# Causal attention, 16 heads: the order of a chunk's key tiles, passed tiles between kept ones

## The reference

```python
a = jax.nn.softmax(jnp.einsum('bhsd,bhtd->bhst', q, k) * D ** (-0.5), axis=-1)
if causal:
    s, t = (a.shape[-2], a.shape[-1])
    mask = (jnp.arange(t)[None, :] > jnp.arange(s)[:, None]).astype(a.dtype)
    a = a * mask
o = jnp.einsum('bhst,bhtd->bhsd', a, v)
```

## Time and profile before

| | us |
|---|---|
| median of 3 runs | 3826.64 |
| lowest and highest | 3819.09 and 3826.94 |
| the profiled execution, its own time | 3808.98 |
| its span, first to last instruction | 3807.2 |
| the stage of the change in it, from the first score to the last copy | 1283.7 to 2207.5 |

### The profile page before, as it was taken

One profiled execution on the slowest core, in us unless ns is written; L12 is line 12 of the kernel. 1 busy time (PEld: TensorE's weight loads), 2 busy tenths in 40 slices (PEclk: granted clock), 3 DMA queues, 4 the chain that ended last, 5 costly groups with the idle time before them and its releaser, 6 DMA issues. The chain is left out here.

```text
span 3807.2 us, 65854 instructions
## 1 busy us (share of the span) xinstructions
PE 3254.3 (85%) x23031; PEld 1440.8 (38%) x23031; DVE 2444.5 (64%) x4118; ACT 1976.2 (52%) x3961; POOL 1482.6 (39%) x795
## 2 busy tenths in 40 slices
PE   4999999526885899999999986599999998969998
PEld 2323332315773232232322254122222222647776
DVE  5878896563114778778788455466666672655665
ACT  2777777331112256666666744156666665523443
POOL 2000000353222231434325240377878777415553
PEclk7989998757996799999999888699999999969999
DMA  1000000286772100100000030100000000347445
GB/s 58 12 14 11 14 8 4 90 302 244 229 240 75 31 16 7 26 5 18 18 5 9 1 109 23 31 18 10 23 10 23 9 10 24 109 145 246 84 82 118
DMA packets 163212, 239.03 MB, mean 63 GB/s; under 512 B 35859, under 2 KB 132826, under 8 KB 155994
## 3 DMA queue, kind: packets, MB, share of 16 engines
q1 hardware_dynamic: 142698, 209.40, 17.4%
q0 software_dynamic: 19056, 24.88, 3.7%
q10 hardware_dynamic: 1152, 0.79, 0.1%
HBM read 136.44 MB, written 68.92 MB: 54 GB/s over the span
## 5 line engine op out<-in xcount | busy, mean ns | idle before, releaser
L1262 DVE TENSOR_REDUCE a_part_max<-a_wb 128x1 f32<-128x512 f32 x1024 | 641.5, 683 | 110.3 <-PE a_wb L1348 101.1
L1814 DVE TENSOR_REDUCE a_part_max<-a_mx 128x2 f32<-128x1024 f32 (+1 forms) x416 | 473.3, 1180 | 264.7 <-PE a_mx L1915 264.7
L1748 ACT ACTIVATE a_e<-a_sc 128x512 f32<-128x512 f32 (+1 forms) x832 | 451.3, 594 | 231.6 <-PE a_sc L1895 225.1
L748 DVE TENSOR_REDUCE xa_part_max<-xa_mx 128x2 f32<-128x802 f32 x512 | 469.7, 985 | 103.4 <-PE xa_mx L845 102.5
L1719 POOL TENSOR_TENSOR a_part_sum<-a_part_sum,a_e 128x2048 f32<-128x2048 f32 x112 | 509.0, 4545 | 53.5 <-ACT a_e L1748 43.4
L1206 ACT ACTIVATE a_e<-a_sc 128x512 f32<-128x512 f32 x640 | 349.4, 601 | 337.7 <-PE a_sc L1373 333.0
L692 ACT ACTIVATE xa_e<-xa_sc 128x512 f32<-128x512 f32 (+1 forms) x832 | 445.8, 596 | 114.1 <-PE xa_sc L832 106.3
L1348 PE MATMUL a_wb<-a_ks,a_qs 96*128 96x512 f16 x1024 | 405.3, 402 | 25.4 <-DVEq L1289 9.5
L1895 PE MATMUL a_sc<-a_qs,a_ks 97*128 97x512 f16 (+1 forms) x832 | 277.3, 397 | 15.5 <-DMA a_qs<-a_neg_max 7.0
L868 PE MATMUL xa_po<-xa_e,xa_v 128*32 128x256 f32 (+1 forms) x3328 | 274.0, 402 | 7.4 <-ACT xa_oc L735 2.6
L1151 POOL TENSOR_TENSOR a_em<-a_e,a_later 128x512 f32<-128x512 f32 x64 | 81.0, 1266 | 459.2 <-ACT a_e L1206 371.9
(11 more groups left out here) (397 smaller groups left out, 5187.9 us busy)
## 6 DMA issues: line engine op xcount, KB each, us to landing
experts_w_up<-in_we SPq DMA_DIRECT2D x32, 1024.0 KB, 6.5
wall<-expert_halves SPq DMA_DIRECT2D x18, 1088.0 KB, 9.8
experts_w_down<-in_we SPq DMA_DIRECT2D x32, 512.0 KB, 6.1
a_qs<-a_stage SPq DMA_DIRECT2D x360, 32.0 KB, 1.8
moe_xr<-sorted_rows SPq DMA_DIRECT2D x79, 136.5 KB, 2.1
a_ks<-a_stage SPq DMA_DIRECT2D x336, 32.0 KB, 1.9
choose_whole<-in_wm SPq DMA_DIRECT2D x18, 544.0 KB, 9.0
expert_halves<-choose_cut SPq DMA_DIRECT2D x18, 544.0 KB, 7.9
```

Source lines behind the costliest of these rows:

```text
L748: dve.tensor_reduce(part_max[:, 2 * h:2 * h + 2, t, c], src[:, :, :mxw], AX.X, ALU.max).then_inc(m_taken, 1)
L1262: dve.tensor_reduce(part_max[:, j, t, k:k + 1], src[:, :mxw], AX.X, ALU.max).then_inc(unit_taken, 1)
L1748: act.activation(e[:r, m % ering, j, :], src[:r, :], ACT.Exp, scale=scale).then_inc(s_taken, 1)
L1814: dve.tensor_reduce(dst, src, AX.X, ALU.max).then_inc(m_taken, 1)
```

## The change

The tiles of a chunk are put in another order, the same for all engines: the passed ones are spread evenly between the kept ones. `tiles` is the list in the new order, `place_of` the place of a tile in it; all waits and ring buffers count by that place. What each tile computes, the rings and the work for the chunks ahead stay. The orders (P passed, K kept): type 0 unchanged; type 1 K P K K K P K K K P K K K P K K; type 2 P K eight times; type 3 P P P K four times.

```diff
+    tiles = []
+    for n in range(NC):
+        skipped = sum(passed(n, kt) for kt in range(nkt))
+        kept = nkt - skipped
+        tiles += sorted(((n, kt) for kt in range(nkt)),
+                        key=lambda x: (2 * x[1] + 1) * kept if x[1] < skipped else (2 * (x[1] - skipped) + 2) * skipped)
+    place_of = {tile: m for m, tile in enumerate(tiles)}
...
-    tile_work = [PASSED_WORK if passed(m // nkt, m % nkt) else TILE_WORK for m in range(nkt * NC + 1)]
+    tile_work = [PASSED_WORK if passed(*tile) else TILE_WORK for tile in tiles] + [TILE_WORK]
...
-                for kt in range(nkt):
-                    if kt == TPC and n - 1 in carry_at:
+                for step, (_, kt) in enumerate(tiles[nkt * n:nkt * n + nkt]):
+                    if step == TPC and n - 1 in carry_at:
                         place_sums(n - 1)
...
-                            pool.wait_ge(pv_done, summed[nkt * before_n + before_kt + 1])
-                        pool.tensor_tensor(em[:, kt % 2, :, :], e[:, (nkt * n + kt) % ering, :, P * i:P * i + P],
+                            pool.wait_ge(pv_done, summed[place_of[before_n, before_kt] + 1])
+                        pool.tensor_tensor(em[:, kt % 2, :, :], e[:, place_of[n, kt] % ering, :, P * i:P * i + P],
...
-            for m in range(nkt * NC):
-                r = kt_rows[m % nkt]
+            for m, (_, kt) in enumerate(tiles):
+                r = kt_rows[kt]
...
-                dve.wait_ge(exp_done, HG * (nkt * n + TPC * (n % NCH)))
+                dve.wait_ge(exp_done, HG * (place_of[n, TPC * (n % NCH) - 1] + 1))
...
             def sum_values(n, kt):
-                m = nkt * n + kt
+                m = place_of[n, kt]
...
-                        sum_values((m - 1) // nkt, (m - 1) % nkt)
+                        sum_values(*tiles[m - 1])
                     elif m:
-                        sum_weights((m - 1) // nkt, (m - 1) % nkt)
+                        sum_weights(*tiles[m - 1])
```

More of the change, by code:

```diff
@@ L971, in passed @@
         return causal and kt < TPC * (n % NCH)
+    tiles = []
[5 more added lines that the diff above has]
+    place_of = {tile: m for m, tile in enumerate(tiles)}
     summed = [0]
-    for m in range(nkt * NC):
-        summed.append(summed[-1] + (not passed(m // nkt, m % nkt)))
+    for tile in tiles:
+        summed.append(summed[-1] + (not passed(*tile)))
     def adds_up(n, kt):
@@ L1145, in _ @@
                     if i is not None:
-                        pool.wait_ge(exp_done, HG * (nkt * n + kt + 1))
+                        pool.wait_ge(exp_done, HG * (place_of[n, kt] + 1))
                         if TPC * n + i >= 2:
                             before_n, before_kt = (n, kt - 2) if i >= 2 else (n - 1, TPC * ((n - 1) % NCH) + i + 2)
-                            pool.wait_ge(pv_done, summed[nkt * before_n + before_kt + 1])
-                        pool.tensor_tensor(em[:, kt % 2, :, :], e[:, (nkt * n + kt) % ering, :, P * i:P * i + P],
+                            pool.wait_ge(pv_done, summed[place_of[before_n, before_kt] + 1])
+                        pool.tensor_tensor(em[:, kt % 2, :, :], e[:, place_of[n, kt] % ering, :, P * i:P * i + P],
                                            later[:, :].unsqueeze(1).to_broadcast([P, HG, P]), ALU.mult).then_inc(masked, 1)
@@ L1154, in _ @@
                         m = nshared[n] + shared[n].index(kt)
-                        pool.wait_ge(exp_done, HG * (nkt * n + kt + 1))
-                        tile = e[:, (nkt * n + kt) % ering, :, :]
+                        pool.wait_ge(exp_done, HG * (place_of[n, kt] + 1))
+                        tile = e[:, place_of[n, kt] % ering, :, :]
                         if m:
@@ L1192, in _ @@
                         act.wait_ge(exp_done, HG * (m - ering + 1))
-                        n, kt = (m - ering) // nkt, (m - ering) % nkt
+                        n, kt = tiles[m - ering]
                         if kt in shared[n]:
                             act.wait_ge(pool_added, nshared[n] + shared[n].index(kt) + 1)
-                    n, kt = m // nkt, m % nkt
+                    n, kt = tiles[m]
                     if passed(n, kt):
@@ L1361, in score @@
             def score(n, kt, j):
-                i = HG * (nkt * n + kt) + j
+                i = HG * place_of[n, kt] + j
                 r = kt_rows[kt]
@@ L1430, in _ @@
             for m in range(nkt * NC + 1):
-                n, kt = m // nkt, m % nkt
-                if kt == 0 and n < NC:
+                n, kt = tiles[m] if m < nkt * NC else (NC, 0)
+                if m % nkt == 0 and n < NC:
                     pe.wait_ge(negmax_loaded, 16 * HG * (n + 1))
```

## The result

| | before | after |
|---|---|---|
| median of 16 runs each, side by side | 3826.79 | 3834.93 |
| lowest and highest | 3813.08 and 3845.80 | 3826.28 and 3858.75 |
| the profiled execution, its own time | 3808.98 | 3832.05 |
| its span | 3807.2 | 3830.2 |
| the stage of the change in it | 924.4 | 940.7 |

The ratio is 1.0035, with an interval of 1.0018 to 1.0052: the change makes the kernel slower by 0.35%, about 13 us (the two medians lie 8.1 apart). The forecast was 3820, no change within 0.2%; the range of 3797 to 3845 holds the time, the direction was wrong. In the profiled executions the stage is 16.3 longer; the other 6.7 of the span's 23.0 lie outside the stage, where by the clock's records PE stood at the lower level for 649 us after and 638 before. The profiled execution of before is faster than any of its 16 runs, so the spans differ by more than the medians.

What follows compares the result with a forecast made beforehand. PE was read as busiest (85%), but in the stage ACT paced passed tiles and PE kept ones. Terms -6.4 (type 1), -7.2 (type 2), +1.5 (type 3), +2 (chunk 15), -6 (clock), +9 (hand-overs) sum to -7.1: 3820, range 3797 to 3845.

Steps and rivals of the forecast that it cites:

- The bound and the two regimes: In the changed stage no engine is full: ACT's exponentials pace passed tiles (PE idle 0.7 each), PE bounds kept tiles.
- First, the gain in type 2: Passed tiles behind kept ones fill PE's 0.7 idle with products and sums: 5.9 us gained per type 2 chunk.
- fourth rival: Products follow a tile later, maxima stay heavier in kept tiles, so the weave doesn't mix; inside the forecast, no own chance.
- Second, the mask's exposure: PE stands 1.0 at diagonal value products, three more times a chunk in types 2 and 3; bounds 0 and 1.5.
- Type 1: Chunks of type 1: gain 3.1 less 1.5 for masks, net -1.6 a chunk, -6.4 for four.
- Type 3: Chunks 3, 7, 11: pairs of kept and passed tiles get longer, net +0.5 a chunk, +1.5 in all.
- Type 0 unchanged (62): Type 0 chunks, whose order is not changed, were to stay at 62 us.
- Chunk 15 (+2): Last chunk: 2 us less at the higher clock, 6 longer at the lower level; +2 was taken.
- Third, the clock: Chunks 2 and 10: even PE load of about 0.8 keeps the clock up, -6; bounds 0 and +6.
- Fourth, the hand-overs: Some 110 more changes of tile kind in the stage, 0.08 us each: +9, ends 0 and 16.
- The third rival: Mask stalls at K0 to K3 in types 2, 3 and chunk 15 outweigh the gain: +15, 3842; chance 0.23.
- The first rival: Weaving pays in full, woven chunks fall to their busiest engine plus edges, type 2 to 50: 3783; chance 0.15.

Runs made afterwards that it cites:

- E15: Kernel before, tile order kept, with PE's weight sums exchanged with value products and the work list dealt by the tile before; 3802.86 in one run.
- E12: Woven kernel with PE's weight sums exchanged with value products and the work list dealt by the tile before; 3789.17 against 3821.89, ratio 0.992.
- E3: Kernel before with the mask of the diagonal blocks left out, so their products don't wait for POOL; 3814.59 in one run.
- E2: Woven kernel with the mask of the diagonal blocks left out, so their products don't wait for POOL; 3807.74 in one run.
- E5: Woven kernel with the diagonal mask left out and the work list dealt by the tile before; 3782.45 in one run.
- E1: Woven kernel with the work list dealt by the tile before, more to tiles behind a kept one; 3833.11 in one run, 3835.03 before beside it.
- E6: Woven kernel with all of type 3, chunk 15 included, back in its old order; 3836.11.
- E4: Woven kernel with chunk 15 alone back in its old order; 3835.04, with 3835.03 of before beside it.
- E10: Woven kernel with PE's weight sums exchanged with value products, list as it is; 3805.63 in one run.
- E11: Kernel before, tile order kept, with PE's weight sums exchanged with value products, list as it is; 3817.62 in one run.

## Why the prediction was wrong, step by step

*The bound and the two regimes* were read rightly: idle time was there to be had, 13.4 us of the stage from E15 to E12.

*First, the gain in type 2 (5.9 a chunk).* This is the step that failed. It took the 0.7 idle of each P as free once P carries K's products, on the busy time of the pair as a whole. The list gives a K its 5.4 maxima and P 3.4, so K's maxima last longer on DVE than K's scores and maxima on PE, and the three PSUM buffers hold no more in advance (no run changed their number). The prediction had the two facts (products follow a tile later, the list is heavier in K) in its fourth rival, as the reason why type 3 gains nothing, and charged type 2 with 0.55 at two pairs. Without mask and with that list the gain is 0.5 (E3 to E2); with the list dealt it is 3.0 (54.3 to 51.3, E3 to E5), still half of what was booked. Over the whole stage weaving without the mask's waits was worth +0.8, no gain at all.

*Second, the mask's exposure (1.0, three more a chunk).* The mechanism was right. Its price hangs on the list. With the list as it is, type 2 loses 2.0 to the mask (55.8 to 53.8) where before lost 0.4 (54.7 to 54.3): 1.6 for three, half of what was booked, because PE is held by DVE anyhow, toward the lower bound that the prediction named. With the list dealt it is 2.9 (54.2 in E1, 51.3 in E5), or 2.5 less before's 0.4, near 3 x 1.0. So type 2 comes out at -0.5 + 1.6 = +1.1 instead of -1.8.

Chunk 14, of type 2 as well, shows how both terms hang on the list. It makes no projections for later chunks, so in it DVE is busy for 36.9 and PE for 44.3, where chunk 10 has 44.8 and 49.5, and PE waits 0.4 for DVE's maxima and 3.8 for masks, where it waits 1.9 and 1.8 in chunk 10. There, at 1.00 in all four kernels, weaving without the mask gains 3.1 (50.5 to 47.4, E3 to E2) and the mask takes 2.7 back (3.1 woven, 0.4 before).

*Type 1* had the right sign: -1.6 forecast, -1.1 at equal clock in three chunks (63.9 to 62.8, where about 62 was said) and nothing in chunk 13. That it came so near is partly luck, as both terms were too large: the gain was 1.9 (63.3 to 61.4, E3 to E2) where 3.1 was booked, the mask 0.8 where 1.5 was.

*Type 3* was forecast at +0.5; it is +2.6, +3.8 and +2.9. The mask is not the whole of it: without it weaving still costs 1.3 and 1.9 in chunks 7 and 11 at equal clock (E3 to E2; 4.0 in chunk 3, which fell from 1.00 to 0.94). The list is part of it: dealt anew it makes chunks 7 and 11 of E1 2.5 and 1.4 shorter than after's at the same clock, 0.94 and 0.93. Lower clock is another: from before to after chunk 3 went from 1.00 to 0.97, chunk 7 from 0.97 to 0.94 and chunk 11 from 0.97 to 0.93. How much each of the three carries is not separated. With mask covered and list dealt type 3 gains 1.6, 0.5 and 1.7 (E15 to E12), of which only chunk 7 is at equal clock.

*Type 0 unchanged (62)* was wrong by 2.3 in chunks 4 and 8 and by 1.3 in chunk 12. The prediction charged the wait of the next chunk's first products to type 3 with 0.4; it is 0.8 and it comes with a wait of 1.2 behind the normalisation (E6).

*Chunk 15 (+2)* came out at +6.7. The direction was right and the size that of its own lower-clock case (+6). The time line of POOL in after, the masks of the chunk's second and third kept tile:

```profile
2195.31 1.26 POOL L1159 TENSOR_TENSOR a_em<-a_e,a_later 128x512 f32<-128x512 f32 x1 [10.72 <-ACT a_e L1214]
...
2207.99 1.26 POOL L1159 TENSOR_TENSOR a_em<-a_e,a_later 128x512 f32<-128x512 f32 x1 [11.42 <-ACT a_e L1214]
```

Four tiles, K P P P, take 12.7 from mask to mask; four passed tiles at ACT's pace would take 9.2. The rest is the P behind K, where PE first stands for the mask and then works off products and sums at the lower clock before the next scores, as its time line shows for the first of these two:

```profile
2196.72 0.68 PE L1407 MATMUL a_po<-a_e,a_v 128*32 128x128 f32 x8 [1.31 <-POOL a_em L1159]
...
2198.72 1.94 PE L1425 MATMUL a_pd<-a_e,ones 128*32 128x512 f32 x8
```

The sums are 1.94 here and 1.04 at the higher clock. Without the mask the chunk still loses 4.1 (47.0 to 51.1, E3 to E2), and the P behind each K still lasts 4.4 where a P at ACT's pace lasts 2.3. So the larger part is the products and sums between the scores. Nor was only K0 exposed here before, as the prediction had it: PE waited for the mask three times in chunk 15 of before, 3.6 in all, against four times and 6.5 after.

*Third, the clock (-6)*. Chunks 2 and 10 went to 1.00 as said. The bound of "+6 if the stalls bring it down elsewhere" came true in part: chunks 3, 6, 7, 11 and 15 now have longer lower stretches. In chunks 1 to 14 PE stood at the lower level for 27.3 us before and 20.5 after. In chunk 2 of before 10.2 us of it cost 3.3 (58.0 against chunk 6's 54.7), so an estimate of the net gain there is 2, not 6. *Fourth, the hand-overs (+9)* were not measured by themselves. Of its two prices the 0.15 from mask to PE stands in rows 8 (1528.41 + 1.27 to 1529.83) and not, as the prediction says, in rows 6, where 0.30 passes (PE still had a maximum to do). Of the sum of -7.1 against +16.3, the misses are 11.4 in type 2 (with its clock), 7.8 in type 3, 5.3 in type 0, 4.7 in chunk 15 and 3.1 in type 1, 32.3 together, and 9 of these had been booked as hand-overs.

*The third rival*, slower by the masks' stalls, named the direction, the place (K0 to K3, with chunk 15) and nearly the time (3842). Its price of 1.5 for each was not what did it in types 1 and 2: there the exposure was cheaper than booked and the gain was missing. *The first rival*, type 2 near 50, is what E12 nearly has (51.2), with both causes removed.

The Trainium skill, Perfetto Trace Analysis, section Optimization Strategy, says that interleaving regimes may improve performance. Here it did so once the wait that the interleaving opens was covered and the side work dealt anew (-13.4 on the stage); the interleaving alone cost 16.3.

## What to carry to other kernels

Before mixing light and heavy tiles, look in which tile the heavy work is really issued: here products follow one tile later, and the order paid most with the side work dealt by the tile *before* (E12). Ask of each step that is moved what used to hide its latency (here weight sums in front of a mask), and move that cover along; and test a gain with the suspected stall taken out entirely, since of two causes that hide behind each other one can look small when it alone is removed, as the list did in E1.

## What was not expected of the hardware

The clock's lower stretches move between chunks that an edit doesn't touch. Added up over chunks 1 to 14 from the clock's records, PE stood at the lower level for 27.3 us before, 20.5 after, 37.5 in E4 and 13.7 in E12. Chunk 10 of after and of E4 is the same program:

```profile
1895.10:1950.90 55.80, 49.49 (x292) 14.84 (x289) 44.78 (x76) 38.46 (x98) 11.73 (x7) 1.00 0.03 8
```

It lasts 55.8 here, at 1.00, and 57.3 in E4, at 0.97. No run controls this; differences of a few us between two stages of one execution each are therefore not read as the effect of an edit, and the claims above rest on chunks at equal clock, on waits, and on stage differences above 10 us. E2 and E3 had the same lower-clock time in chunks 1 to 14, 23.9 each; the 7.7 of E1 and the 3.5 between E10 and E11 are the least certain figures of the tables.
